# Layer norms 5 and 6 of a two-layer decoder in halves by batch, and the last products between turned rows

## The chip, the cores and the metric

The kernel runs on one core of a Trainium2 chip. The metric is the device time of one execution in microseconds. A core has a matrix engine (TensorE, PE), a vector engine (DVE), a scalar engine (ScalarE, ACT), GpSimd (POOL) and a queue of transfers (SyncE, SP); each works through its own list of instructions in order and waits on semaphores.

## The reference

`x` is 8 batches of 128 rows by 512 columns, in fp32. Six sublayers are added to it, each over a layer norm:

```
def _layernorm(x, axis=-1, eps=1e-05):
    m = jnp.mean(x, axis=axis, keepdims=True)
    v = jnp.var(x, axis=axis, keepdims=True)
    return (x - m) / jnp.sqrt(v + eps)
...
    x = x + _L0_attn_ref(_layernorm(x, axis=-1), ...)
    x = x + _L0_xattn_ref(_layernorm(x, axis=-1), ctx_4096, mask_BxSxS2_bk0, fside_Bx32xSxS2_0, ...)
    x = x + _L0_ffn_ref(_layernorm(x, axis=-1), ...)
    x = x + _L1_attn_ref(_layernorm(x, axis=-1), ...)
    x = x + _L1_xattn_ref(_layernorm(x, axis=-1), ctx_4096, ctx_4096, ...)
    x = x + _L1_ffn_ref(_layernorm(x, axis=-1), ...)
```

The fifth sublayer is a cross attention with 32 heads of 16 columns (8 key groups of 4 heads), scores, softmax and an output product. The sixth unpacks a 512x512 weight from 3 bits, multiplies the normed x with it and adds a bias. The fourth ends with a root mean square norm over the attention output, applied here as one scale per row (`y_scale`).

## The kernel before

**Numbers as pairs.** Every operand of a large product is split in a rounded high part and the low rest. `mm3` makes a product of three matmuls: high by high, high by low, low by high. A product of 128 rows by 512 columns over K = 512 is thus 12 matmuls. ScalarE writes a high part (`hi`, `turned`, `weight_hi`), the vector engine subtracts it for the low part (`lo`); for weights in SBUF, GpSimd does that (`split_lo`, one instruction over 128x1024).

**Layer norms** are numbered 0 to 5 in the code; the title's fifth and sixth are 4 and 5. Before, norms 4 and 5 run whole. `stats` (bn_stats) is taken per batch after its addition; when all eight are there, `deviation` makes eight aggregations and one `var_eps`, ScalarE the square root, the vector engine the reciprocal (`normed`). Then for each batch b: the vector engine writes the normed row block to one of two buffers (`probs` 0 and 1), TensorE turns it (four transposes in a bank `pj`, `turn`), ScalarE writes `xt_hi`, the vector engine `xt_lo`, which frees the bank. Norms 1 to 3 already go in halves of four batches (`half_deviation`, `half_rstd`); their order is written out by hand.

**Order of the end of the fourth sublayer (L883 to L932, L1281 to L1292, L1868 to L1887).** TensorE finishes the last head pair between the key and value products of the fifth: `tail`, `sums` (the sum of squares per row), `keys(hf, m)`, four transposes of the values. The vector engine adds `y_scale` times y to x (`add_scaled`, one per batch). GpSimd sums the squares of two heads (`both_heads`), splits weights of slots 3, 0, 1, 2 and 4, then makes the first two blocks of masked keys (`block_keys`), and behind the last addition clears and fills the padded values. TensorE then turns rows 0 to 3, makes `queries(0, 0)`, turns rows 4 and 5, `queries(0, 1)`, rows 6 and 7, `queries(0, 2)`, `scores(0)`, `queries(0, 3)`.

**The loop of the fifth sublayer** has 16 iterations n (batch n // 2, half of the key groups n % 2), each with four groups g: scores of iteration n + 1 (TensorE), `row_max` (vector), `exps` (ScalarE), `row_sums` and reciprocal (vector), `normalise` (GpSimd), `transposes` (TensorE), `turned_out` (ScalarE), `values` (TensorE). In even n from 2 on `output(n // 2 - 1)` is a product of 12 matmuls, added to x by the vector engine with its bn_stats (`add`); in odd n `heads` copies the attention output as a pair. `block_keys(n + 2)` is the last GpSimd instruction but the padding in an iteration. `dequantise(part)` makes a quarter of the 3 bit weight in three vector instructions (0 and 1 before the loop, 2 and 3 in iterations 0 and 1). Weights of `l1x_o` (slot 3) get their low part on the vector engine in front of the first row sums.

**The end (L1043 to L1056).** After values(15) TensorE turns the weight's quarters 0 and 1 (`turned_weights`), makes output(7), turns quarters 2 and 3, then all eight rows of norm 5, and then eight products, each added to x by the vector engine and sent out by the SP queue. Two banks `ou` alternate. The bias is added for all batches ahead of the first product's addition:

```
            normed(5)
            for b in range(B):
                dve.tensor_tensor(X[:, b, :], X[:, b, :], BIAS[:], ALU.add).then_inc(bias_added, 1)
            for b in range(B):
                n, bank = nth(OU["l1f"], 0, 0, b)
                dve.wait_ge(bias_added, b + 1)
                add_output(n, bank, X[:, b, :])
```

Of the kernel before, what the change touches and what calls it, by code (L numbers as in the profile page):

```python
# [92 lines left out]
LNV = [0, 1, 3, 5, 7, 8]  # L93
# [15 lines left out]
def build(nc, a):  # L109
    ctx = ExitStack()  # L110
    with ctx:
# [280 lines left out]
        def _(pool):  # L392
# [96 lines left out]
            split_lo(4, SLOT["l1x"][4])  # L489
# [27 lines left out]

            block_keys(0)
            block_keys(1)
            pool.wait_ge(la_y, B)  # L520
# [4 lines left out]
            pad_values(0)  # L525
            for g in range(KG):
                normalise(0, g)
# [10 lines left out]
        def _(pe):  # L538
# [392 lines left out]
            keys(1, 0)  # L931
            pe.wait_ge(la_v, 3)  # L932
            keys(1, 1)

# [75 lines left out]

            def turned_weights(c):
# [9 lines left out]
            turn(4, range(0, 4))  # L1021
# [4 lines left out]
            turn(4, range(4, 6))  # L1026
            queries(0, 1)
            turn(4, range(6, B))
            queries(0, 2)
            scores(0)  # L1030
            queries(0, 3)
            for n in range(NG):
# [6 lines left out]
                if n % 2 == 0 and n:  # L1039
                    output(n // 2 - 1)  # L1040
                values(n)
                for c in {5: (0,), 6: (1,), 7: (2, 3)}.get(n, ()):
                    queries(1, c)  # L1043
            turned_weights(0)
            turned_weights(1)
            output(B - 1)
            turned_weights(2)
            turned_weights(3)
            layer_norm(5)
            for b in range(B):  # L1050
                n, bank = nth(OU["l1f"], 0, 0, b)
                pe.wait_ge(pj_done, PJ["ln5"] + b + 1)
                ou_free(n)
                for c in range(KC):
                    last = mm3(ou[bank][:], rows(XT, b)(c), wrows(L1F_SLOTS)(c), c == 0, c == KC - 1)
                last.then_inc(ou_full, 1)  # L1056
# [3 lines left out]
        def _(act):  # L1060
# [220 lines left out]
            scale_std(1)  # L1281
# [3 lines left out]
            deviation(4)  # L1285
            for f in range(2):
                n, bank = nth(PJ["l1xv"], 0, 0, 2 + f)
                act.wait_ge(pj_full, n + 1)
                act.activation(AF[:, V1 + f * HALF:V1 + (f + 1) * HALF], pj[bank][:], ACT.Copy).then_inc(pj_done, 1)
            act.wait_ge(kr_full, 2)  # L1290
# [35 lines left out]
            turned(4, range(6))  # L1326
            queries(0, 0)
            turned(4, range(6, B))
            queries(0, 1)
            queries(0, 2)  # L1330
# [23 lines left out]
            for g in range(KG):  # L1354
                turned_out(NG - 1, g)
            heads(B - 1)

# [7 lines left out]
            deviation(5)  # L1365
            weights_hi(2)
            weights_hi(3)
            turned(5, range(B))
# [3 lines left out]
        def _(dve):  # L1372
# [495 lines left out]
            for n in range(HB):  # L1868
# [7 lines left out]
                l1a_step(None, (HG - 1, 1), "O", n)  # L1876
            for b in range(HB):
                stats(b)
            mean_square(1)
            scaled(1)  # L1880
            for b in range(HB, B):
                add_scaled(b)
# [34 lines left out]
            for g in range(KG):  # L1917
                row_max(0, g)
# [125 lines left out]
```

## Time and profile before

| | us |
|---|---|
| median of three runs | 2473.59 (2472.96 to 2476.45) |
| the profiled execution | 2473.39 |
| its span | 2471.6 |
| PE busy | 2366.2 |
| DVE busy | 1256.2 |
| ACT busy | 902.2 |
| POOL busy | 668.5 |

The profile comes from one execution. Busy times are shares of the span from the first to the last instruction; matmuls are pipelined, so a busy TensorE isn't one at its peak. In a row of the timeline, "idle" in brackets is how long the engine did nothing before it, and behind the arrow stands what ended that. The granted clock is TensorE's, as a share of 2.4 GHz; 0.50 is 1.2 GHz.

### The profile page before, as it was taken

How to read it: one execution, taken by the hardware profiler on the slowest of the kernel's cores; microseconds unless marked ns; L12 is line 12 of the kernel's file. 1: busy time of each engine (PE TensorE's matmuls, PEld its weight loads, DVE VectorE, ACT ScalarE, POOL GpSimd, SP SyncE). 2: the span in 40 equal slices, each digit the busy share in tenths (PEclk: the TensorE clock that was granted, in tenths of full speed). 3: DMA queues.
4: the chain of work that ended last, by engine and by line, in shares of the span. 5: the costliest groups of instructions: out<-in, count | busy, mean ns of one | idle time of the engine just before them, and what ended most of it. 6: DMA issues, size and time to landing. Idle time of an engine off the chain costs nothing.

```text
span 2471.6 us, 38446 instructions
## 1 busy us (share of the span) xinstructions
PE 2366.2 (96%) x13227; PEld 2019.0 (82%) x13227; DVE 1256.2 (51%) x2917; ACT 902.2 (37%) x2230; POOL 668.5 (27%) x383
## 2 busy tenths in 40 slices
PE   5999899999999999998999999999999999997888
PEld 3788688888888889887888888888888888886555
DVE  6444644445444444456644444444444444457765
ACT  2111344444444444443233333333333333334763
POOL 4434522322222322231311111111111111112550
PEclk9999999999999999999999999999999999998888
DMA  3110212111111211110111111111111111100000
GB/s 117 68 43 26 103 52 74 61 51 58 61 51 60 76 51 51 68 60 27 49 41 45 45 45 45 45 45 45 45 45 45 45 45 45 45 18 0 1 1 35
DMA packets 36831, 118.96 MB, mean 48 GB/s; under 512 B 4904, under 2 KB 7336, under 8 KB 36784
## 3 DMA queue, kind: packets, MB, share of 16 engines
q1 hardware_dynamic: 36784, 118.35, 14.1%
q8 instruction: 28, 0.46, 0.1%
q14 instruction: 19, 0.16, 0.0%
HBM read 116.24 MB, written 2.10 MB: 48 GB/s over the span
## 4 chain that ended last, share of the span: by engine, by line
PE 87%; DVE 6%; issue 3%; POOL 2%; ACT 1%; SPq 0%; DMA 0%; POOLq 0%; ACTq 0%; DVEq 0%
PE pj L542 19%; PE pj L543 18%; PE pj L544 18%; PE ou L542 6%; PE ou L544 6%; PE ou L543 6%; PE pv L720 2%; PE sc L857 2%; PE pv L866 2%; PE sc L704 2%; PE tp L711 1%; POOL w_lo L410 1%; DVE neg_max L1891 1%; POOL w_hi L408 1%; DVE probs L1424 1%
## 5 line engine op out<-in xcount | busy, mean ns | idle before, releaser
L402 POOL TENSOR_TENSOR w_lo<-raw,w_hi 128x1024 fp32r<-128x1024 f32 x145 | 346.6, 2391 | 1438.0 <-ACT w_hi L1094 1398.6
L542 PE MATMUL pj<-xt_hi,w_hi 128*128 128x512 f32 x1232 | 498.8, 405 | 6.2 <-DVE xt_lo L1459 2.4
L543 PE MATMUL pj<-xt_lo,w_hi 128*128 128x512 f32 x1232 | 482.1, 391 | 0.0
L544 PE MATMUL pj<-xt_hi,w_lo 128*128 128x512 f32 x1232 | 481.7, 391 | 0.0
L542 PE MATMUL ou<-w_hi,act_hi 128*128 128x512 f32 x684 | 274.7, 402 | 0.8 <-DVE x L1383 0.6
L542 PEld LDWEIGHTS pj<-xt_hi,w_hi 128*128 128x128 f32 x1232 | 233.0, 189 | 50.0 <-DVE xt_lo L1459 2.6
L544 PEld LDWEIGHTS pj<-xt_hi,w_lo 128*128 128x128 f32 x1232 | 232.0, 188 | 49.5
L544 PE MATMUL ou<-w_hi,act_lo 128*128 128x512 f32 x684 | 267.6, 391 | 0.0
L543 PE MATMUL ou<-w_lo,act_hi 128*128 128x512 f32 x684 | 266.8, 390 | 0.0
L543 PEld LDWEIGHTS pj<-xt_lo,w_hi 128*128 128x128 f32 x1232 | 233.0, 189 | 40.8
L1383 DVE TENSOR_TENSOR x<-x,ou 128x512 f32<-128x512 f32 x192 | 130.8, 684 | 254.6 <-PE ou L544 254.2
L1245 ACT ACTIVATE side<-pj 128x512 f32<-128x512 f32 (+1 forms) x256 | 125.6, 491 | 341.1 <-PE pj L544 341.0
L1821 DVE TENSOR_TENSOR queries_keys<-side,pj 128x512 f32<-128x512 f32 x128 | 88.1, 688 | 184.6 <-ACT side L1245 184.6
L1160 ACT ACTIVATE queries_keys<-pj 128x512 f32<-128x512 f32 x128 | 76.5, 598 | 245.2 <-PE pj L544 245.2
L542 PE MATMUL pj<-w_hi,xt_hi 128*128 128x256 f32 (+1 forms) x544 | 160.7, 295 | 2.5 <-DVE x_sum L1461 1.6
L1094 ACT ACTIVATE w_hi<-raw 128x1024 fp32r<-128x1024 f32 x146 | 153.5, 1051 | 20.5 <-PE ou L544 18.7
L542 PEld LDWEIGHTS ou<-w_hi,act_hi 128*128 128x128 f32 x684 | 128.9, 188 | 36.6 <-issue 10.7
L543 PE MATMUL pj<-w_lo,xt_hi 128*128 128x256 f32 (+1 forms) x544 | 157.4, 289 | 0.0
L544 PE MATMUL pj<-w_hi,xt_lo 128*128 128x256 f32 (+1 forms) x544 | 157.4, 289 | 0.0
L544 PEld LDWEIGHTS ou<-w_hi,act_lo 128*128 128x128 f32 x684 | 128.7, 188 | 27.8
L543 PEld LDWEIGHTS ou<-w_lo,act_hi 128*128 128x128 f32 x684 | 129.0, 189 | 24.4
L542 PE MATMUL pj<-w_hi,ctx_hi 128*128 128x256 f32 x512 | 147.8, 289 | 0.7 <-POOL w_lo L410 0.7
(241 smaller groups left out, 4553.1 us busy)
## 6 DMA issues: line engine op xcount, KB each, us to landing
raw<-in_l1a_w SPq DMA_DIRECT2D x80, 512.0 KB, 4.2
raw<-in_l0x_w SPq DMA_DIRECT2D x64, 512.0 KB, 4.3
side<-in_side SPq DMA_DIRECT2D x32, 512.0 KB, 3.9
raw<-in_ffn_w SPq DMA_DIRECT2D x15, 512.0 KB, 3.3
raw<-in_l0f_w SPq DMA_DIRECT2D x6, 512.0 KB, 3.7
raw<-in_l1x_w SPq DMA_DIRECT2D x6, 512.0 KB, 3.8
raw<-in_taylor_w SPq DMA_DIRECT2D x5, 512.0 KB, 7.3
x<-in_x SPq DMA_DIRECT2D x2, 1024.0 KB, 6.6
```

Of the source, the lines that this page charges most:

```text
L402: pool.tensor_tensor(WL[:, s, :], RAW[:, s, :], f32(WH[:, s, :]), ALU.subtract).then_inc(w_ready[s], 1)
L542: pe.matmul(out, wh, xh, start=first, stop=False)
L543: pe.matmul(out, wh, xl, start=False, stop=False)
L544: return pe.matmul(out, wl, xh, start=False, stop=last)
L704: last = pe.matmul(score(j)[:, h * S:(h + 1) * S], heads_of(0, h, j), heads_of(1, h, j), start=True, stop=True)
L720: last = pe.matmul(pv[:, h * S:(h + 1) * S], VT[:, n, h * S:(h + 1) * S], TA[:, n % 2, h * S:(h + 1) * S], start=True, stop=True)
L857: last = pe.matmul(score(j)[:, h * S:(h + 1) * S], heads_of(1, h, j), heads_of(0, h, j), start=True, stop=True)
L1094: act.activation(WH[:, s, :], RAW[:, s, :], ACT.Copy).then_inc(w_hi[s], 1)
L1160: act.activation(QK[:, n, :], bank[:], ACT.Copy, scale=S ** -0.5 if n < 2 else 1.0).then_inc(pj_done, 1)
L1245: act.activation(F[:, x % 2, 0:w], pj[bank][:, 0:w], ACT.Sigmoid).then_inc(la_sg, 1)
L1383: dve.tensor_tensor(dst, dst, ou[bank][:], ALU.add).then_inc(x_done, 1)
L1821: dve.tensor_tensor(dst, F[:, x % 2, 0:w], pj[bank][:, 0:w], ALU.mult).then_inc(pj_done, 1)
```

## The change

Norms 4 and 5 get two halves of four batches each. `LNV`, the count of deviations before each norm, becomes `[0, 1, 3, 5, 7, 9]`. On TensorE:

```diff
             keys(1, 0)
+            turn(4, range(2))
             pe.wait_ge(la_v, 3)
             keys(1, 1)
+            turn(4, range(2, HB))
...
+            def product(b):
+                bank = (b + 1) % 2
+                pe.wait_ge(pj_done, PJ["ln5"] + b + 1)
+                if b:
+                    pe.wait_ge(x_done, OU["l1f"] + b - 1)
+                else:
+                    pe.wait_ge(tn_out, NG * KG)
+                for c in range(KC):
+                    last = mm3(ou[bank][:], rows(XT, b)(c), wrows(L1F_SLOTS)(c), c == 0, c == KC - 1)
+                last.then_inc(ou_full, 1)
...
-            turn(4, range(0, 4))
             pe.wait_ge(pj_done, PJ["ln4"] + HB)
...
             queries(0, 0)
-            turn(4, range(4, 6))
             queries(0, 1)
-            turn(4, range(6, B))
+            turn(4, range(HB, HB + 2))
             queries(0, 2)
+            turn(4, range(HB + 2, B))
             scores(0)
...
                     output(n // 2 - 1)
+                if n + 1 == NG:
+                    turned_weights(0)
+                    turned_weights(1)
                 values(n)
...
-            turned_weights(0)
-            turned_weights(1)
-            output(B - 1)
             turned_weights(2)
             turned_weights(3)
-            layer_norm(5)
+            turn(5, range(2))
+            output(B - 1)
             for b in range(B):
...
+                if b + 2 < B:
+                    turn(5, (b + 2,))
+                product(b)
```

On GpSimd the split of slot 4 moves behind the first padding, and both key blocks behind all eight additions:

```diff
             split_lo(2, SLOT["l1x"][2])
-            split_lo(4, SLOT["l1x"][4])
...
+            pool.wait_ge(la_y, B)
             block_keys(0)
             block_keys(1)
-            pool.wait_ge(la_y, B)
...
             pad_values(0)
+            split_lo(4, SLOT["l1x"][4])
             for g in range(KG):
                 normalise(0, g)
```

On ScalarE:

```diff
-            scale_std(1)
             act.wait_ge(kr_full, 1)
             for m in range(2):
                 keys_out(0, m)
-            deviation(4)
+            half_deviation(4, 0)
+            scale_std(1)
...
+            turned(4, range(HB))
             act.wait_ge(kr_full, 2)
...
-            turned(4, range(6))
             queries(0, 0)
-            turned(4, range(6, B))
+            half_deviation(4, 1)
             queries(0, 1)
+            turned(4, range(HB, B))
             queries(0, 2)
...
-            for g in range(KG):
-                turned_out(NG - 1, g)
-            heads(B - 1)
-
+            turned_out(NG - 1, 0)
+            turned_out(NG - 1, 1)
+            half_deviation(5, 0)
+            turned_out(NG - 1, 2)
+            turned_out(NG - 1, 3)
...
             weights_hi(1)
-            deviation(5)
+            heads(B - 1)
             weights_hi(2)
             weights_hi(3)
-            turned(5, range(B))
+            turned(5, range(3))
+            half_deviation(5, 1)
+            turned(5, range(3, B))
```

On the vector engine, at norm 4 (`turn_row` writes a normed row, `turn_lo` the low part of a turned one):

```diff
-                l1a_step(None, (HG - 1, 1), "O", n)
+                if n < HB - 1:
+                    l1a_step(None, (HG - 1, 1), "O", n)
...
             for b in range(HB):
                 stats(b)
+            half_deviation(4, 0)
+            l1a_step(None, (HG - 1, 1), "O", HB - 1)
             mean_square(1)
+            half_rstd(4, 0)
+            turn_row(4, 0)
+            turn_row(4, 1)
             scaled(1)
-            for b in range(HB, B):
-                add_scaled(b)
+            add_scaled(4)
+            turn_lo(4, 0)
+            turn_row(4, 2)
+            turn_lo(4, 1)
+            turn_row(4, 3)
+            add_scaled(5)
+            turn_lo(4, 2)
+            turn_lo(4, 3)
+            add_scaled(6)
+            add_scaled(7)
             for b in range(HB, B):
                 stats(b)
-            deviation(4)
-
-            normed(4)
+            half_deviation(4, 1)
+            half_rstd(4, 1)
+            turn_row(4, 4)
+            turn_row(4, 5)
+            turn_lo(4, 4)
...
```

Around the loop and at the end:

```diff
             dequantise(0)
-            dequantise(1)
             for g in range(KG):
                 row_max(0, g)
+            for g in range(KG):
+                row_sums(0, g)
             dve.wait_ge(w_hi[3], SLOT["l1x_o"] + 1)
             dve.tensor_tensor(WL[:, 3, :], RAW[:, 3, :], f32(WH[:, 3, :]), ALU.subtract).then_inc(w_ready[3], 1)
-            for g in range(KG):
-                row_sums(0, g)
...
-                if n in (0, 1):
-                    dequantise(2 + n)
+                if n in (0, 1, 3):
+                    dequantise((0, 1, 3).index(n) + 1)
...
+                if n + 2 == NG:
+                    half_deviation(5, 0)
                 row_sums(n + 1, 2)
...
-            heads(B - 1)
...
+            half_rstd(5, 0)
+            turn_row(5, 0)
+            turn_row(5, 1)
             weights_lo(0)
             weights_lo(1)
+            heads(B - 1)
             weights_lo(2)
             weights_lo(3)
+            turn_lo(5, 0)
+            turn_row(5, 2)
+            turn_lo(5, 1)
+            turn_row(5, 3)
+            add(B - 1)
+            half_deviation(5, 1)
+            turn_lo(5, 2)
+            half_rstd(5, 1)
+            turn_row(5, 4)
+            add_bias(0)
+            add_bias(1)
+            turn_lo(5, 3)
+            turn_row(5, 5)
+            add_product(0)
+            turn_lo(5, 4)
+            turn_row(5, 6)
+            add_bias(2)
+            add_product(1)
...
```

and so on, one low part, one row, one bias and one product a step, to `add_product(7)`.

## Rows read from the trace of the kernel before

**Rows 1.** The page, part 1: busy us (share of the span) and instructions.
```profile
PE 2366.2 (96%) x13227; PEld 2019.0 (82%) x13227; DVE 1256.2 (51%) x2917; ACT 902.2 (37%) x2230; POOL 668.5 (27%) x383
```
**Rows 2.** Table by stage: us, busy PE, PEld, DVE, ACT, POOL, clock, DMA.
```profile
2240.00:2256.00 16.00, 8.67 (x37) 6.42 (x35) 14.18 (x30) 5.41 (x12) 6.44 (x8) 0.79 0.00 1
```
**Rows 3.** Timeline, all engines, norm 4 to scores(1): start, us, engine, line, operation.
```profile
2238.01 2.46 DVE L1866 BATCH_NORM_STATS2 bn_stats<-x 128x6 f32<-128x512 f32 x4
2238.53 4.75 POOL L402 TENSOR_TENSOR w_lo<-raw,w_hi 128x1024 fp32r<-128x1024 f32 x2 [1.60 <-ACT w_hi L1094]
...
2241.01 5.52 DVE L1861 SCALAR_TENSOR_TENSOR x<-y,y_scale,x 128x512 f32<-128x512 f32 x4
...
2250.92 1.97 PE L565 MATMUL pj<-identity,probs 128*128 128x128 f32 x8 [6.36 <-DVE probs L1424]
...
2257.09 0.79 PE L542 MATMUL ou<-xt_hi,w_hi 128*128 128x512 f32 x1 [1.41 <-DVE xt_lo L1377]
...
2262.38 1.36 PE L565 MATMUL pj<-identity,probs 128*128 128x128 f32 x8
...
2266.31 1.04 PE L565 MATMUL pj<-identity,probs 128*128 128x128 f32 x8
...
2271.71 1.28 ACT L1309 ACT_TABLE_LOAD   x1
...
2280.00 0.80 PE L967 MATMUL sc<-keys_blocked,act_whole 32*128 32x256 f32 x2
```
**Rows 4.** Timeline of GpSimd in the loop: the key blocks.
```profile
2280.85 0.61 POOL L497 TENSOR_TENSOR keys_blocked<-keys_whole,block_mask 128x256 f32<-128x256 f32 x1
...
2302.07 0.61 POOL L497 TENSOR_TENSOR keys_blocked<-keys_whole,block_mask 128x256 f32<-128x256 f32 x1
...
2310.26 0.61 POOL L497 TENSOR_TENSOR keys_blocked<-keys_whole,block_mask 128x256 f32<-128x256 f32 x1
...
2326.40 0.61 POOL L497 TENSOR_TENSOR keys_blocked<-keys_whole,block_mask 128x256 f32<-128x256 f32 x1
```
**Rows 5.** Timeline of the last stage, all engines.
```profile
2421.58 0.60 ACT L1318 ACTIVATE turned_whole<-tp 128x512 f32<-128x512 f32 x1 [1.38 <-PE tp L981]
...
2423.23 1.77 PE L995 MATMUL pv<-turned_whole,values_padded 128*32 128x512 f32 x8 [0.69 <-ACT turned_whole L1318]
...
2424.93 1.97 PE L1018 MATMUL pj<-identity,w 128*128 128x128 f32 x8
...
2429.74 0.69 DVE L1383 TENSOR_TENSOR x<-x,ou 128x512 f32<-128x512 f32 x1 [1.49 <-PE ou L544]
...
2434.91 1.97 PE L565 MATMUL pj<-identity,probs 128*128 128x128 f32 x8 [4.33 <-DVE probs L1424]
...
2468.48 0.69 DVE L1383 TENSOR_TENSOR x<-x,ou 128x512 f32<-128x512 f32 x1 [2.03 <-PE ou L544]
```
**Rows 6.** Vector engine by line, 2434 to 2472: busy us, mean ns, idle.
```profile
L1377 DVE TENSOR_TENSOR xt_lo<-pj,xt_hi 128x512 fp32r<-128x512 f32 x8 | 5.5, 689 | 1.4 <-ACT xt_hi L1064 1.2
...
L1951 DVE TENSOR_TENSOR x<-x,bias 128x512 f32<-128x512 f32 x8 | 4.9, 684 | 0.0
L1424 DVE TENSOR_SCALAR probs<-x,bn_mean_var,rstd 128x512 f32<-128x512 f32 x8 | 4.3, 542 | 1.2 <-PE pj L565 1.2
```
**Rows 7.** Timeline of vector engine and GpSimd at norm 1.
```profile
256.55 0.38 DVE L1437 BATCH_NORM_AGGREGATE bn_mean_var<-bn_stats 128x2 f32<-128x6 f32 x4
256.96 1.03 DVE L1441 TENSOR_SCALAR var_eps<-bn_mean_var 128x4 f32<-128x4 f32 x1
...
256.08 1.88 POOL L416 TENSOR_TENSOR ctx_hi<-side,one 128x1024 fp32r<-128x1024 f32 x1
```
**Rows 8.** Table by single us, columns as in rows 2.
```profile
2422.00:2423.00 1.00, 0.54 (x4) 0.30 (x4) 0.00 (x0) 0.60 (x2) 0.00 (x0) 1.00 0.00 0
2423.00:2424.00 1.00, 0.77 (x8) 0.16 (x8) 0.00 (x0) 0.17 (x1) 0.00 (x0) 0.73 0.00 0
...
2447.00:2448.00 1.00, 1.00 (x5) 0.78 (x5) 1.00 (x3) 0.00 (x0) 0.00 (x0) 0.83 0.00 0
```

More of the change, by code:

```diff
@@ L1043, in _ @@
                     queries(1, c)
-            turned_weights(0)
-            turned_weights(1)
-            output(B - 1)
             turned_weights(2)
             turned_weights(3)
-            layer_norm(5)
+            turn(5, range(2))
+            output(B - 1)
             for b in range(B):
[L1051 to L1056, printed above, removed]
+                if b + 2 < B:
+                    turn(5, (b + 2,))
+                product(b)
         @block.scalar
@@ L1940, in weights_lo, with add_bias, add_product @@
                 lo(fill, HI["l1f"] + c, wpair(WL, L1F_SLOTS, c, 512), pj[fill[1]][:], wpair(WH, L1F_SLOTS, c, 512))
+            def add_bias(b):
+                dve.wait_ge(ln_x, 5 * B + b + 1)
+                dve.tensor_tensor(X[:, b, :], X[:, b, :], BIAS[:], ALU.add).then_inc(bias_added, 1)
+            def add_product(b):
+                dve.wait_ge(bias_added, b + 1)
+                add_output(OU["l1f"] + b, (b + 1) % 2, X[:, b, :])
+            half_rstd(5, 0)
+            turn_row(5, 0)
+            turn_row(5, 1)
             weights_lo(0)
             weights_lo(1)
-            add(B - 1)
-            dve.wait_ge(x_done, OU["l1f"])
-            deviation(5)
+            heads(B - 1)
             weights_lo(2)
             weights_lo(3)
-            normed(5)
-            for b in range(B):
-                dve.tensor_tensor(X[:, b, :], X[:, b, :], BIAS[:], ALU.add).then_inc(bias_added, 1)
-            for b in range(B):
-                n, bank = nth(OU["l1f"], 0, 0, b)
-                dve.wait_ge(bias_added, b + 1)
-                add_output(n, bank, X[:, b, :])
+            turn_lo(5, 0)
[16 more added lines that the diff above has]
+            add_product(1)
+            turn_lo(5, 5)
+            turn_row(5, 7)
+            add_bias(3)
+            add_product(2)
+            turn_lo(5, 6)
+            add_bias(4)
+            add_product(3)
+            turn_lo(5, 7)
+            add_bias(5)
+            add_product(4)
+            add_bias(6)
+            add_product(5)
+            add_bias(7)
+            add_product(6)
+            add_product(7)
 def arr(a):
```

16 lines of the change are left out of this document (15 added, 1 removed).

## The prediction

> **What bounds the kernel now.** I read the page first: TensorE is busy 96% of the span [rows 1]. The change touches nothing before 2215 us, though, so this average says little. The table by stage shows where TensorE isn't the bound [rows 2]: around layer norm 4 (the code's number) it is busy 8.67 of 16 us, the vector engine 14.18. Then the timeline of the first stage [rows 3], to see who releases whom: TensorE is idle for 6.36 us, from 2244.56 until the first turned row at 2250.92, and once more before the queries (2257.09), of which the first product then takes 5.3 us, until 2262.38. The reader sees that the vector engine holds it up: its four additions end at 2246.5, and four statistics, aggregation, deviation and rows follow. Then the loop by GpSimd's key blocks, one an iteration [rows 4], and the last stage [rows 5]: TensorE waits 4.33 us for row 0, turns eight rows in 10 us at the half clock and at the pace of a ring (turn, high part, low part, next row), and only then makes eight products at a pitch of 2.72 us (the 2.03 and 0.69 of the last row).
>
> All times are on the clock of the profiled execution: 2473.39 us for a span of 2471.6, 0.2 us under the median of 2473.59. The 1.8 us around the span and the 3.1 from the last addition to its end I take as unchanged.
>
> **Stage 1, layer norm 4 in halves.** Removed is the one norm behind all additions; added are two half norms with a deviation each. In order:
> - The first four statistics start at 2238.01 behind a y addition, which moves behind them: now 2237.4 to 2239.9, and with four aggregations 2240.35 [rows 3, 7]. Next is var_eps, while GpSimd splits slot 2 (2238.53 to 2240.9, half of its row). Such an instruction waits until GpSimd's ends [rows 7]: 2241.0.
> - y addition (0.7) and mean square: 2241.95; reciprocal and rows 0, 1 (0.54 each, [rows 6]): 2243.15. TensorE turns them between keys(1,0) and keys(1,1) (2.8 us each, so from 2241.7 on), by 2243.65; keys(1,1) ends at 2246.45 and rows 2 and 3 at 2247.35, 0.45 a row and less at full clock (the 1.04 for two).
> - High part 0.6, low part 0.69, the second low part 0.7 behind: 2248.95. queries(0,0) starts there instead of at 2257.09 and takes 2.8 us at full clock; with queries(0,1) 2254.5.
> - GpSimd's split of slot 4 and its two key blocks are out of the additions' way: two SBUF inputs cost them 1.38 each there, 0.70 free. The last ends at 2250.3, the statistics at 2252.75, the aggregation at 2253.1.
> - But GpSimd starts at 2250.3 as well: two key blocks (0.61 each when alone, [rows 4]), two clears and two paddings (1.2 in all), and split_lo(4), 2.4 us, from about 2252.75 to 2255.15. The second var_eps comes at 2253.1 and is held until 2255.2. These 2 us lie on the path.
> - Root, reciprocal, rows 4 and 5: 2256.7; turned 2257.2; queries(0,2) to 2259.95; rows 6 and 7 turned by 2260.85; last low part 2262.3, for which scores(0) waits, now as then.
> - ScalarE copies queries(0,2) and makes a weight (1.05), so its table load starts at 2263.3 against 2271.71, and the first exponentials at 2264.85. The row sums follow at once, no longer behind w_lo (1.2 us). GpSimd's second normalisation ends at 2270.05, and scores(1) starts at 2270.8 against 2280.00: **9.2 us gained** at the loop's door. w_lo(3) has its reader two iterations on. dequantise(1) stood ahead of the first maxima, but under the table load: taking it away there gains nothing.
>
> Bounds: half clock for queries(0,0) (2.5) and the turned rows (1.2): 5.5. No hold, and scores(1) 0.7 sooner: 11.8.
>
> **Stage 2, the loop.** dequantise stands in iterations 0, 1 and 3, not 0 and 1. Two iterations with it take 21.22 us (key blocks at 2280.85 and 2302.07), two without 16.14 (2310.26 and 2326.40): 2.54 each, of which the half clock may have a part. Two of its three instructions last 0.69 as in [rows 6]; with 1.4 the lower end. I take 2.5 lost; the upper end is 3.1. half_deviation(5,0) puts 0.55 us before the last two row sums of iteration 14; stage 3 carries it. GpSimd is idle at that point.
>
> **Stage 3, the end.** On the old axis:
> - The 0.55 moves the last two normalisations to 2421.4 and 2422.4. ScalarE's root, with a table load (1.28), fills 2420.2 to 2421.7, inside the 1.38 us that it idles before a copy [rows 5]; that copy is ready at 2422.1. Hidden; without that idle time 1.5.
> - turned_weights(0) and (1) go ahead of values(15). At the half clock, as now [rows 5, 8], they take 1.97, to 2425.1; values(15), ready at 2423.8, ends at 2426.9.
> - heads(7) ends at 2428.15 on the vector engine, and the low parts of weights 2 and 3 are queued behind it: 2428.85, 2429.5. Rows 0 and 1 need their banks, and are turned by 2429.35 and 2430.0. Behind them on TensorE stands output(7): to 2432.8, now 2429.7. Three us given up.
> - Row 2 is turned at 2433.25, and product(0) starts there, not at 2444.5. A product costs 2.73 and a turned row 0.45: 3.2 us a step up to product(5) at 2449.25, then 2452.0, 2454.7, end 2457.45, while the last addition now starts at 2468.48, 0.1 behind its product. Ten us of turning become 6 x 0.45.
> - The vector engine's work of a step is 0.69+0.54+0.61+0.69 = 2.5 of 3.2 us [rows 5, 6], so hidden. But there is a ring: product(b) ends, row b+3 is turned (0.45), high (0.6), low (0.69), next row, bias and addition (1.85), and after 3.65 to 3.8 us product(b+2) may write the bank, where TensorE arrives after 3.65. I charge 0.2 in all: 10.9 - 0.2 = **10.7 us gained**, the 0.55 included.
>
> Bounds: half clock over output(7) (2.4) and 0.15 a step in the ring: 7.5. Full clock at the turned weights (1.5): 12.2.
>
> **Sum.** 9.2 - 2.5 + 10.7 = 17.4; 2473.39 - 17.4 = 2456.0 us. The worst ends give 5.5 - 3.1 + 7.5 = 9.9 (2463.5), the best 11.8 - 1.4 + 12.2 = 22.6 (2450.8).
>
> **Rivals.**
> A. split_lo(4) doesn't hold var_eps, because it starts behind it: 1.9 more, **2454.1**. For it: the two starts are 0.35 us apart. Against: what GpSimd does ahead of the split is as long as four statistics. 10%.
>
> B. The clock falls in the gaps. It fell at 2423.3, after a stretch in which TensorE worked in pieces (0.54 of the last us), and at 2249, idle since 2244.56; it returned at 2447.2, the engine at work since 2443 [rows 3, 8]. The new stage 1 has gaps of 1.6 and 1.8 us, the new end 1.2. At the half clock queries(0,0) costs 2.5 more and output(7) 2.4: **2460.9**. 25%. The Trainium skill, TensorE: Matmul & The Clock Gate, in its section on the second failure mode of the gate, says that short idles between groups of matmuls can make the clock go up and down. By that rule both losses come; the row at 2423 is in line with it. The gap that cost the clock in stage 1 was 6.36 us long, though, and hence no more than 25%.
>
> C. The ring of stage 3 is slower: a pitch of 3.8 instead of 3.2 us over six products, 3.6 more: **2459.6**. For it: less than 0.1 us of slack a step. Against: the bias is free to run ahead. 10%.
>
> D. Slower than before: turning in between keeps the half clock over the products. One then costs 5.1 instead of 2.73 (queries(0,0) took 5.3), a row 1.0 instead of 0.45: 8 x 2.4 + 6 x 0.55 = 22.5 more, **2478.5**. It decides from the sixth such product on (17.4 / 2.95). Against: TensorE has work without a gap there, and in the same place it came back 2.8 us into the products [rows 8]. 2%.
>
> E. The first half of layer norm 4 comes no earlier than all eight rows now, since eight instructions stand ahead of it: stage 1 gives nothing, so 8.2 in all, **2465.2**. Against: its rows are due at 2243.15, 7 us before today's. 3%.
>
> My sum has the other 50%.
>
> **Numbers.** Forecast 2456.0; from 2451.0, the best ends, to 2463.0, which holds A, B and C and leaves out D, E and some of the worst ends. A measurement of this kernel can tell about 0.2%, 5 us: faster by more (under 2468.6) 0.95, within it 0.03, slower 0.02.
>
> **What would show it.** queries(0,0) near 2249 at 0.23 us a matmul; the second var_eps lasting 2 us beside split_lo(4); the table load near 2263; iteration 3 some 2.5 us longer. At the end eight products at 3.2 us, the first at 2426.6 (2433.25 less 9.2 plus 2.5). It is wrong if queries(0,0) lasts 5 us, if the pitch is over 3.4, or if scores(1) comes less than 6 us earlier.

## The result and the profile after

| | before | after |
|---|---|---|
| median of the executions (each over 4) | 2473.28 us (2470.65 to 2476.45) | 2458.77 us (2455.03 to 2460.19) |
| the profiled execution | 2473.39 us | 2459.67 us |
| its span | 2471.6 us | 2457.8 us |

The ratio is 0.9932, with a 95% interval of 0.9920 to 0.9945: 16.8 us faster by the ratio, 14.5 by the medians. Four more executions of the changed kernel, in a later run, gave 2456.30 us (2453.91 to 2456.72) and 0.9925 (0.9908 to 0.9941). The forecast was 2456.0 us.

The page of after has the same load on every engine but TensorE, as it should, for no product was added or taken away (part 1, answers to [rows 1]); what went is idle time and time at the half clock.

```profile
PE 2358.6 (96%) x13227; PEld 2012.9 (82%) x13227; DVE 1255.9 (51%) x2921; ACT 902.7 (37%) x2232; POOL 668.3 (27%) x383
```

The two profiled executions are 4.26 us apart before the first changed instruction: the split of slot 1 (GpSimd's w_lo behind its first sum of squares) starts at 2218.49 before and at 2222.75 after. So I read every stage from that split on, not from the span's start. The timeline of stage 1 after, all engines, answers to [rows 3, 7]:

```profile
2244.56 0.63 DVE L1455 TENSOR_SCALAR var_eps<-bn_mean_var 128x4 f32<-128x4 f32 x1
...
2246.72 1.11 PE L565 MATMUL pj<-identity,probs 128*128 128x128 f32 x8 [0.64 <-ACT act_whole L1299]
...
2253.05 0.50 PE L542 MATMUL ou<-xt_hi,w_hi 128*128 128x512 f32 x1 [1.57 <-DVE xt_lo L1391]
...
2256.66 2.38 POOL L402 TENSOR_TENSOR w_lo<-raw,w_hi 128x1024 fp32r<-128x1024 f32 x1
...
2257.14 1.92 DVE L1455 TENSOR_SCALAR var_eps<-bn_mean_var 128x4 f32<-128x4 f32 x1
...
2260.15 1.11 PE L565 MATMUL pj<-identity,probs 128*128 128x128 f32 x8 [1.37 <-DVE probs L1896]
...
2266.56 0.48 PE L969 MATMUL sc<-keys_blocked,act_whole 32*128 32x256 f32 x2 [1.67 <-DVE xt_lo L1391]
...
2267.03 1.28 ACT L1320 ACT_TABLE_LOAD   x1
```

The reader sees the 6.36 us wait of TensorE gone: rows 0 and 1 are turned 0.64 us after TensorE came free, and the waits left are 1.57, 1.37 and 1.67. The second var_eps, an instruction over four columns, lasts 1.92 us, to the end of GpSimd's split. The table of the 16 us around the norm, the same stretch as in [rows 2] moved by 4.26, has TensorE busy 12.41 us instead of 8.67, at full clock:

```profile
2244.26:2260.26 16.00, 12.41 (x61) 9.60 (x61) 14.52 (x33) 5.83 (x13) 5.47 (x8) 1.00 0.00 1
```

GpSimd's key blocks in the loop after, against [rows 4]: from the first to the third 20.01 us (21.22 before), from there to the fifth 17.21 (16.14 before, from the fourth block to the sixth).

```profile
2277.35 0.61 POOL L496 TENSOR_TENSOR keys_blocked<-keys_whole,block_mask 128x256 f32<-128x256 f32 x1
...
2297.36 0.61 POOL L496 TENSOR_TENSOR keys_blocked<-keys_whole,block_mask 128x256 f32<-128x256 f32 x1
...
2306.57 0.61 POOL L496 TENSOR_TENSOR keys_blocked<-keys_whole,block_mask 128x256 f32<-128x256 f32 x1
...
2314.57 0.61 POOL L496 TENSOR_TENSOR keys_blocked<-keys_whole,block_mask 128x256 f32<-128x256 f32 x1
```

The end after, all engines, answers to [rows 5]. L1031 are the turned weights, L997 is values(15), L565 the turned rows:

```profile
2417.59 1.28 ACT L1087 ACT_TABLE_LOAD   x1
...
2418.88 0.21 ACT L1087 ACTIVATE std<-var_eps 128x4 f32<-128x4 f32 x1
...
2420.23 1.04 PE L1031 MATMUL pj<-identity,w 128*128 128x128 f32 x8
...
2421.20 1.06 PE L997 MATMUL pv<-turned_whole,values_padded 128*32 128x512 f32 x8
...
2424.46 1.23 PE L565 MATMUL pj<-identity,probs 128*128 128x128 f32 x8 [0.90 <-DVE w_lo L1391]
...
2428.30 0.60 PE L565 MATMUL pj<-identity,probs 128*128 128x128 f32 x4
...
2431.51 0.60 PE L565 MATMUL pj<-identity,probs 128*128 128x128 f32 x4
...
2437.91 0.60 PE L565 MATMUL pj<-identity,probs 128*128 128x128 f32 x4
...
2441.30 0.60 PE L565 MATMUL pj<-identity,probs 128*128 128x128 f32 x4
...
2453.59 0.69 DVE L1397 TENSOR_TENSOR x<-x,ou 128x512 f32<-128x512 f32 x1 [2.03 <-PE ou L544]
```

The turned weights take 1.04 us, not 1.97. The wait of 4.33 us is 0.90, and the eight rows no longer stand together: one is turned every 3.21 us with a product between, once 3.39. The vector engine by line, 2420 to 2455, against [rows 6]: the same instructions at the same price, with more idle time ahead of the low parts (5.4 us) and none ahead of the bias or the rows.

```profile
L1391 DVE TENSOR_TENSOR xt_lo<-pj,xt_hi 128x512 fp32r<-128x512 f32 x8 | 5.5, 689 | 5.4 <-ACT xt_hi L1074 5.4
L1990 DVE TENSOR_TENSOR x<-x,bias 128x512 f32<-128x512 f32 x8 | 5.4, 684 | 0.0
L1896 DVE TENSOR_SCALAR probs<-x,bn_mean_var,rstd 128x512 f32<-128x512 f32 x7 | 3.8, 538 | 0.0
```

The table by single us has the clock at full in the very stretch where it fell before [rows 8] (the columns as there):

```profile
2418.00:2419.00 1.00, 0.26 (x2) 0.26 (x3) 0.32 (x2) 0.99 (x2) 1.00 (x2) 1.00 0.00 0
2421.00:2422.00 1.00, 1.00 (x11) 0.19 (x9) 0.45 (x1) 1.00 (x3) 0.00 (x0) 1.00 0.00 0
2425.00:2426.00 1.00, 1.00 (x8) 0.89 (x8) 0.25 (x1) 0.87 (x2) 0.00 (x0) 1.00 0.00 0
```

### The profile page after: what moved, and what is told of

It is laid out like the page before. It is cut to its first block, busy times and chain, and to the rows that moved or that the text cites. A ratio compares the mean times of both kernels' runs of the same rounds, so it can differ in the third digit from the quotient of the medians.

```text
span 2457.8 us, 38454 instructions
## 1 busy us (share of the span) xinstructions
PE 2358.6 (96%) x13227; PEld 2012.9 (82%) x13227; DVE 1255.9 (51%) x2921; ACT 902.7 (37%) x2232; POOL 668.3 (27%) x383
## 4 chain that ended last, share of the span: by engine, by line
PE 88%; DVE 5%; issue 3%; POOL 2%; ACT 1%; SPq 0%; DMA 0%; POOLq 0%; ACTq 0%; DVEq 0%
PE pj L542 19%; PE pj L543 19%; PE pj L544 19%; PE ou L542 6%; PE ou L544 6%; PE ou L543 6%; PE pv L720 2%; PE sc L857 2%; PE pv L866 2%; PE sc L704 2%; PE tp L711 1%; POOL w_lo L410 1%; POOL w_hi L408 1%; PE sc L969 1%; DVE neg_max L1938 1%
## 5 line engine op out<-in xcount | busy, mean ns | idle before, releaser
L544 PEld LDWEIGHTS pj<-xt_hi,w_lo 128*128 128x128 f32 x1232 | 232.6, 189 | 49.7
L1104 ACT ACTIVATE w_hi<-raw 128x1024 fp32r<-128x1024 f32 x146 | 153.5, 1052 | 20.5 <-PE ou L544 18.7
L542 PEld LDWEIGHTS ou<-w_hi,act_hi 128*128 128x128 f32 x684 | 128.7, 188 | 36.6 <-issue 10.7
```

What stands on the lines that cost most here:

```text
L542: pe.matmul(out, wh, xh, start=first, stop=False)
L544: return pe.matmul(out, wl, xh, start=False, stop=last)
L1104: act.activation(WH[:, s, :], RAW[:, s, :], ACT.Copy).then_inc(w_hi[s], 1)
```

## The experiments

I cut every profiled execution at four instructions: the start of the split of slot 1, the first matmul of scores(1), GpSimd's first normalisation for values(15) (2416.78 before, 2414.15 after), and the last addition. "Half" is the time in the stage with TensorE at the half clock, worked out from the tables by single us as twice the sum of 1 minus the granted clock.

```
kernel                        split at  start  loop (half)   end (half)  rest
before                        2218.49   61.51  136.78 44.5  51.70 17.0    3.1
before, again                 2221.69   61.42  135.05 34.1  50.92 13.7    3.1
changed                       2222.75   52.72  138.68 49.8  39.44  0.0    4.2
changed, again                2219.66   52.75  138.41 49.5  39.44  0.0    4.2
norm 4 alone                  2220.65   52.73  138.57 49.7  51.67 17.1    3.1
norm 5 and end alone          2217.83   61.43  134.99 34.1  40.78  3.4    3.1
split of slot 4 late          2218.43   50.65  134.85 34.1  41.01  3.4    3.1
GpSimd's old order            2219.73   52.56  138.41 49.5  39.45  0.0    3.8
quarters in 5, 7, 9           2219.58   52.79  138.52 49.5  39.44  0.0    3.1
quarter 0 in the gap          2221.88   54.07  135.61 37.6  40.76  3.4    3.1
weights behind values(15)     2221.47   52.74  138.63 49.7  44.06  6.8    3.1
rows ahead of the products    2219.48   52.74  138.42 49.5  44.96  3.4    3.1
late split, 5, 7, 9           2219.63   50.68  137.08 44.4  39.43  0.0    3.1
late split, quarter in gap    2220.50   56.51  138.11 49.1  39.43  0.0    3.1
```

**Both kernels once more.** No edit.

> The changed kernel, unchanged. Theory: the gain of 13.7 us in the first profiled pair is 18.1 by stages (8.8 up to scores(1), -1.9 in the loop, 11.2 at the end) less 4.26 us by which the profiled execution was late already at 2218 us, and that lateness is chance: a second profiled execution has GpSimd's first split w_lo (L402, behind both_heads of the last pair) anywhere from 2217 to 2224 us, while the three stages repeat within 0.3 us each. Rival: the change itself costs 4 us ahead of its own place (a longer program); then the split starts at 2222.5 to 2223.5 again.

> The kernel before, unchanged, for its own spread. In the profiled execution of before the loop took 136.78 us with TensorE's clock at half for 44.5 us; the kernel with only the end changed, whose code is the same up to iteration 14, took 134.99 with 34.1. Theory: which stretches of the loop run at half is settled from execution to execution by small shifts, so this one has any of 34, 37, 41 or 44 us at half, and 134.9 to 136.9 for the loop in step. Rival: it is fixed by the kernel; then 136.7 to 136.9 and 44.5 again. Start 61.5 and end 51.7 in both.

Measured: 2456.30 us for the changed kernel and 2474.19 for the one before, which is 1.0001 (0.9991 to 1.0011) of itself. The changed kernel's three stages repeat to 0.3 us, and the split is at 2219.66 this time. For the kernel before it is at 2221.69, later than at first. The 4 us ahead of the change are chance, and the rival that the change costs them falls. The end of the kernel before took 50.92 us this time, not the 51.7 expected, with 3.3 us less at the half clock. On its loop the theory holds: with not a line changed it took 135.05 us with 34.1 at half, against 136.78 with 44.5. The table by single us of this second execution shows where they part, 7 us into the loop:

```profile
2289.00:2290.00 1.00, 0.53 (x8) 0.16 (x8) 1.00 (x2) 1.00 (x5) 0.00 (x0) 0.96 0.00 0
2290.00:2291.00 1.00, 1.00 (x8) 0.00 (x0) 0.93 (x5) 1.00 (x6) 0.63 (x1) 0.50 0.00 0
2293.00:2294.00 1.00, 1.00 (x14) 0.71 (x15) 0.00 (x0) 0.66 (x2) 1.00 (x2) 0.83 0.00 0
2295.00:2296.00 1.00, 0.62 (x6) 0.38 (x4) 1.00 (x3) 0.78 (x3) 0.00 (x0) 1.00 0.06 16
```

The clock falls at 2290 and is back at 2293.3. In the first execution, 3.2 us earlier throughout, the same fall came at 2287 and lasted until 2293.7.

**Norm 4 alone, norm 5 alone.** The first has norm 5 whole and the old end, the second the old start:

```diff
@@ norm 4 alone: TensorE, and the other engines alike
-                if n + 1 == NG:
-                    turned_weights(0)
-                    turned_weights(1)
...
+            layer_norm(5)
@@ norm 5 alone: the vector engine, and the other engines alike
-            half_deviation(4, 0)
...
+            deviation(4)
+            normed(4)
```

> Norm 4 in halves, GpSimd's order and dequantise as in the changed kernel; norm 5 whole and the end as in the kernel before. Theory (stages add up): 8.8 - 1.9 = 6.9 us faster than before, about 2466.5 to 2467; from the last normalisation but one to the end 51.7 us as before. Rival 1: the end isn't independent (the clock at the end hangs on norm 4's side or the halves of norm 5 overlap what was won): the end takes 2 us more or less than 51.7. Rival 2: the lateness at 2218 us comes with the new end's instructions; then it is gone here.

> Start of the fifth sublayer, norm 4, dequantise and GpSimd's order as in the kernel before; norm 5 in halves, turned weights ahead of values(15) and the products between turned rows as in the changed kernel. Theory: 11.2 us faster than before, about 2462; the end 40.5 us. Rival: the full clock at the turned weights (the changed kernel has 0.99 there, the kernel before 0.5) hangs on the loop's phase; then the turned weights take 1.97 us instead of 1.04 and the end is 41.5 to 43 us: 2463 to 2464.5.

Measured: 2469.05 us, 0.9978 (0.9967 to 0.9988), 5.6 less than before (6.9 expected); and 2461.60 us, 0.9951 (0.9934 to 0.9967), 13.1 less. Together 18.7, where the whole change gave 18.4 against the same executions of before. The parts add up. Norm 4 alone has start 52.73 and the old end of 51.67: its rivals fall. Norm 5 alone wins by more than the 11.2 expected. Between its profile and the first of before, the end gives 10.9 us and the loop 1.8, in which it ran at half for only 34.1 us. The turned weights ran at half, as the rival has it, but the end of 40.78 stays close to the theory's 40.5 and under the rival's 41.5 to 43 (timeline of TensorE in that kernel):

```profile
2420.93 1.83 PE L1029 MATMUL pj<-identity,w 128*128 128x128 f32 x8
```

**The split of slot 4.**

```diff
@@ late split
             pad_values(0)
+            pool.wait_ge(ln_x, 5 * B)
             split_lo(4, SLOT["l1x"][4])
@@ GpSimd's old order
             split_lo(2, SLOT["l1x"][2])
+            split_lo(4, SLOT["l1x"][4])
...
-            pool.wait_ge(la_y, B)
             block_keys(0)
             block_keys(1)
+            pool.wait_ge(la_y, B)
```

> The changed kernel, but GpSimd waits for the deviation of norm 4's second half before it splits slot 4. Theory: var_eps took 1.92 us only because GpSimd's split (2.38 us) held it; now it takes 0.1 to 0.2, rows 4 to 7 and scores(0) come 1.7 us sooner, and as slot 4 isn't needed before output(0) nothing waits for the split unless it holds the first normalisation: scores(1) 1.0 to 1.7 us sooner on the axis of the first split. Rival 1: the 1.9 us are hidden behind queries(0,1) (TensorE idled only 1.37 us there), so 0.5 to 1.4. Rival 2: the split, now from 2257.3 to 2259.7, holds the next two-input work of the vector engine instead, no gain (within 0.3).

> The changed kernel with GpSimd's order as before: split of slot 4 right behind slot 2, key blocks ahead of the wait for the additions. Theory of the prediction: the second var_eps is no longer held (1.9 us less), but the rows 0 and 1 of the first half are now beside the split (they start 1.2 to 1.6 us later) and two of the additions beside the key blocks (0.7 more each), so scores(0) comes -0.7 to +1.0 us against the 43.8 after the first split. Rival: the hold is all there is to it, 1.7 us earlier, as in the kernel whose split comes late. Rival 2: the additions' 0.7 and the rows come all on the path: 1.5 to 3 us later.

The late split is released by norm 4's last row, not by its deviation, as the expectation has it. The timeline of that kernel:

```profile
2252.84 0.17 DVE L1456 TENSOR_SCALAR var_eps<-bn_mean_var 128x4 f32<-128x4 f32 x1
...
2257.89 2.35 POOL L402 TENSOR_TENSOR w_lo<-raw,w_hi 128x1024 fp32r<-128x1024 f32 x1 [5.49 <-DVE probs L1897]
```

The same var_eps takes 0.17 us, scores(0) starts 1.66 us sooner after the first split (42.19 against 43.85), and scores(1) 2.10 sooner, more than the 1.0 to 1.7 expected; the last 0.4 of it go with 1.7 us of half clock ahead of scores(1), which this kernel lacks. That the hold lies on the path is shown. The median is 2450.32 us, 0.9907 (0.9888 to 0.9925), 6.0 under the changed kernel on the same chip. That is more than the 2.1. Between the spans of the two profiled executions 6.3 us are 1.2 ahead of the cut, 2.1 in the start, 3.6 in the loop and 1.0 in the rest, less 1.6 in the end: the loop's half clock lasted 34.1 us instead of 49.5, while not a line of it was changed.

GpSimd's old order gave 2456.00 us (0.9928, 0.9913 to 0.9943), within 0.2 us of the changed kernel at every cut. Its timeline shows the hold at another place:

```profile
2239.74 4.72 POOL L402 TENSOR_TENSOR w_lo<-raw,w_hi 128x1024 fp32r<-128x1024 f32 x2 [1.58 <-ACT w_hi L1104]
...
2242.95 2.55 DVE L1896 TENSOR_SCALAR probs<-x,bn_mean_var,rstd 128x512 f32<-128x512 f32 x2
...
2255.51 0.17 DVE L1455 TENSOR_SCALAR var_eps<-bn_mean_var 128x4 f32<-128x4 f32 x1
```

Rows 0 and 1 end at 2245.5 with the split of slot 4's own end at 2244.46 in between: 2.55 us instead of 1.00. The second var_eps is free. What one half wins the other pays, so reordering GpSimd's list as the change did brought nothing by itself (0.2 us the other way).

The Trainium skill, in SBUF — State Buffer, section "SBUF: two separate sides", has the vector engine and GpSimd share one pair of ports, which is locked for a whole instruction, and not divided. The rows agree: 1.92 and 0.63 us for an instruction that takes 0.17 alone, each up to the end of GpSimd's.

**The quarters of the 3 bit weight.** The prediction charged the loop 2.5 us for one more quarter in it.

```diff
@@ quarters in 5, 7, 9
-                if n in (0, 1, 3):
-                    dequantise((0, 1, 3).index(n) + 1)
+                if n in (5, 7, 9):
+                    dequantise((5, 7, 9).index(n) + 1)
@@ quarter 0 in the gap
             turn_row(4, 7)
+            dequantise(0)
             turn_lo(4, 6)
...
-            dequantise(0)
+            dequantise(1)
...
-                if n in (0, 1, 3):
-                    dequantise((0, 1, 3).index(n) + 1)
+                if n in (0, 1):
+                    dequantise(2 + n)
```

> The changed kernel, its quarters 1, 2 and 3 of the 3 bit weight in iterations 5, 7 and 9 instead of 0, 1 and 3. Theory of the prediction: one quarter costs its iteration 2.5 us, so the key blocks of iterations 0 to 2 come 16.2 to 17 us apart instead of 19.9 and those of iterations 5, 7 and 9 each 2.5 us later than now. Second theory, from the runs so far (with the clock at half for 34.1 us of the loop the kernel with two quarters inside took 134.99 us and the one with three 134.85; with 44.5 and 49.5 us at half 136.78 and 138.41): a quarter costs under 0.4 us anywhere, the first iterations are long for another reason and stay at 19.3 to 20.5 us together, and the loop differs from 138.4 only with the time at the half clock.

> The changed kernel, with quarter 0 of the 3 bit weight in a gap of the vector engine ahead of norm 4's row 6, quarter 1 ahead of the loop, 2 and 3 in iterations 0 and 1. By the prediction's term (2.5 us for a quarter in the loop) the loop falls to 136 us and the total by 1.5 to 2.2 us. By the second theory (a quarter costs nothing there) the start changes by -0.3 to +0.5 us and the loop by no more than its time at the half clock brings (0.2 to 0.35 us for each us).

Quarters in iterations 5, 7 and 9: 2454.23 us, 0.9916 (0.9900 to 0.9933). The loop takes 138.52 us, as with the quarters in 0, 1 and 3, and the first iterations stay long without them (GpSimd's key blocks, 19.79 us from the first to the third):

```profile
2274.24 0.61 POOL L496 TENSOR_TENSOR keys_blocked<-keys_whole,block_mask 128x256 f32<-128x256 f32 x1
...
2294.03 0.61 POOL L496 TENSOR_TENSOR keys_blocked<-keys_whole,block_mask 128x256 f32<-128x256 f32 x1
```

The term of the prediction falls. Quarter 0 in the gap: 2456.92 us, 0.9927 (0.9910 to 0.9944), no gain. Its loop is 2.8 us shorter, which alone would look like the 2.5; but the table by stage of the loop tells of another cause. One row for each execution, from scores(1) to the normalisation. The kernel before, with two quarters inside:

```profile
2280.00:2416.78 136.78, 112.55 (x716) 71.88 (x716) 99.40 (x200) 96.78 (x302) 69.85 (x85) 0.84 0.00 1
```

The same kernel again:

```profile
2283.11:2418.16 135.05, 108.39 (x714) 69.73 (x714) 99.45 (x200) 97.09 (x302) 69.81 (x86) 0.87 0.00 1
```

Norm 5 and the end alone, two quarters as well:

```profile
2279.26:2414.25 134.99, 108.40 (x714) 69.71 (x714) 99.45 (x200) 97.08 (x302) 69.80 (x85) 0.87 0.00 1
```

And the late split, with three:

```profile
2269.08:2403.93 134.85, 108.64 (x714) 69.90 (x714) 102.50 (x206) 97.16 (x302) 71.22 (x87) 0.87 0.00 1
```

With the clock at 0.87 the loop takes 134.99 and 135.05 us with two quarters and 134.85 with three, though the vector engine is 3 us busier. At 44.5 us of half clock it is 136.78 with two and 137.08 with three; at 49.1 to 49.8 it is 138.11 with two and 138.4 to 138.7 with three. A quarter costs -0.2 to +0.6 us; each us at the half clock costs (138.41 - 134.85) / 15.4 = 0.23.

In the gap kernel, the start is 1.3 us longer, which neither theory had. The first exponentials are only 0.4 us later; what is late is the copy of queries(0,3) (2271.64, 49.76 after the split, against 47.98), whose product fell under a half clock from 2266.3 on.

**Both ideas together.**

> The changed kernel with the late split of slot 4 and the quarters of the weight in iterations 5, 7 and 9. Theory: a quarter costs nothing wherever it stands, so this equals the kernel with the late split alone: start 50.65, loop 134.9 (34 us at half), end 39.4 to 41, 2450 to 2452 us. Rival: the 134.85 us of that kernel was an accident of one execution: loop 138.4 and 49.5 us at half as in all five kernels with the same start but one, 2453 to 2455.

> Late split of slot 4 with quarter 0 in the vector engine's gap, quarter 1 ahead of the loop, 2 and 3 in iterations 0 and 1. Theory: start 50.65 + 1.3 (quarter 1 delays the first maxima, as it did in the kernel with the gap) = 52.0, loop 134.8 to 135.7 at 34 to 38 us of half clock, end 39.4 to 40.8: 2451 to 2453. Rival (the prediction's term of 2.5 us a quarter): the loop 2.5 us shorter than with the late split alone, 132.4: 2448 to 2450.

Late split with the quarters in 5, 7 and 9: 2453.96 us over 5 executions (2448.81 to 2457.46), 0.9917 (0.9904 to 0.9931). The start repeats (50.68). The loop does neither: 137.08 us with 44.4 at half, between theory and rival, and the five times spread over 8.6 us. The 34.1 of the late split alone weren't fixed by its code. Over both kernels with the late split, nine executions have a median of 2452.4 us; the sixteen of the three with a start of 52.6 to 52.8 us and the new end in full (the changed one, GpSimd's old order, quarters in 5, 7 and 9) 2456.2. The granted clock over the whole of each execution is on record, and orders the five times: 0.991 for 2448.81 us, 0.988 for 2452.42 and 2453.96, 0.987 for 2454.45, 0.985 for 2457.46. At equal clock, from 0.987 to 0.990, the kernels with the late split lie 1.1 to 5.2 us under those three by their medians, 2.3 at 0.990. So I take some 2 us of the 3.8 as shown (stage 1), the rest as the clock's luck; whether the earlier start helps the clock isn't shown.

Late split with quarter 0 in the gap: 2459.69 us, 0.9941 (0.9927 to 0.9954), worse than either, and outside both expectations. The timeline of that kernel shows why:

```profile
2260.00 2.47 POOL L402 TENSOR_TENSOR w_lo<-raw,w_hi 128x1024 fp32r<-128x1024 f32 x1 [5.57 <-DVE probs L1897]
...
2260.29 2.73 DVE L1517 TENSOR_TENSOR w<-w,q_norm 128x512 f32<-128x512 f32 x1
```

The split, freed by the last row, starts just before the product w times q_norm that I had put behind that row, and holds it for 2 us ahead of the low part that scores(0) needs: 44.59 instead of 42.19. In the longer gap the clock fell (8.9 us at half in the start, none in the late split alone), and scores(1) is 5.9 us late.

**The end.**

```diff
@@ weights behind values(15)
-                if n + 1 == NG:
-                    turned_weights(0)
-                    turned_weights(1)
                 values(n)
...
+            turned_weights(0)
+            turned_weights(1)
             turned_weights(2)
@@ rows ahead of the products
+            turn(5, range(2, B))
             for b in range(B):
-                if b + 2 < B:
-                    turn(5, (b + 2,))
                 product(b)
```

> The changed kernel, with the weight's quarters 0 and 1 turned behind values(15), as before. Theory: the two now fill a wait of TensorE for the copy that values(15) reads (0.7 to 1.0 us), so the end grows by 0.7 to 1.1 us, at the full clock. Rival: in that wait the clock falls, as in the kernel before, and the turned weights and output(7) run at half: 1.0 for the weights and up to 2.4 for the product on top, the end 3 to 4.5 us longer.

> The changed kernel, but all rows of norm 5 are turned ahead of the first product; halves and early weights as they are. Theory: six rows (2 to 7) go by the ring of turn, high part, low part over two banks, 1.2 to 1.3 us each, so the first product starts 6.5 us later while each step loses its 0.45 of turning: the end 3.5 to 5 us longer than 39.4. Rival: with TensorE in pieces for 7 us the clock falls, as in the kernel before, and comes back only some us into the products: 8 to 11 us longer. Third: the halves alone brought the gain, and the alternation is worth under 1 us.

Weights behind values(15): 2461.80 us, 0.9945 (0.9929 to 0.9962), the end 4.6 us longer with 6.8 at half. It is the rival, just above its 3 to 4.5, though what ran at half was values(15) and turned blocks, and not output(7). The fastest of the four executions, 2457.30 us, had a granted clock of 0.990, the others 0.985 to 0.987: the loss isn't in every execution. TensorE's timeline in that kernel:

```profile
2419.76 1.94 PE L997 MATMUL pv<-turned_whole,values_padded 128*32 128x512 f32 x8 [0.69 <-ACT turned_whole L1328]
...
2421.63 1.70 PE L1031 MATMUL pj<-identity,w 128*128 128x128 f32 x8
...
2424.16 1.25 PE L1031 MATMUL pj<-identity,w 128*128 128x128 f32 x8 [0.83 <-DVE w_lo L1390]
...
2426.31 1.93 PE L565 MATMUL pj<-identity,probs 128*128 128x128 f32 x8 [0.90 <-DVE w_lo L1390]
```

The wait of 0.69 us that the turned weights had filled is back, values(15) and the first weights run at half, the rows 0 and 1 once more. But the second execution of before had the same wait of 0.69 and its values(15) at full clock (1.06 us), and norm 5 and the end alone had the wait filled and its weights at half. Over all fourteen profiles, the four without the filling have the fall at values(15) in three, whose loops ran at half for 44.5 to 49.7 us, and not in the one with 34.1. The ten with it have the fall at the weights in the three with 34.1 to 37.6 us, and not in the seven with 44.4 to 49.8. So whether the clock falls there goes with the loop's pattern as well as with the filling, and the filling doesn't forbid it.

Rows ahead of the products: 2460.35 us, 0.9945 (0.9928 to 0.9962), the end 5.5 us longer with 3.4 at half. TensorE's timeline there:

```profile
2424.75 1.04 PE L565 MATMUL pj<-identity,probs 128*128 128x128 f32 x8
...
2428.30 0.66 PE L565 MATMUL pj<-identity,probs 128*128 128x128 f32 x4 [2.51 <-DVE probs L1895]
...
2429.35 0.66 PE L565 MATMUL pj<-identity,probs 128*128 128x128 f32 x4 [0.40 <-DVE probs L1895]
...
2430.82 2.17 PE L565 MATMUL pj<-identity,probs 128*128 128x128 f32 x8 [0.81 <-DVE probs L1895]
```

TensorE waits 3.72 us in all for row 4 (behind the second half's deviation) and those after it, and the clock falls at 2431 for the last two. The theory's 3.5 to 5 is just missed; the third view, that the alternation is worth under 1 us, falls. Of the end's 12.3 us, the alternation holds 5.5 and the early weights 4.6, each measured with the other present, in one profile each, and with the half clock that came with it (3.4 and 6.8 us).

## Why the prediction came out right, point by point

The cuts give for the two profiled executions 8.8 (start) - 1.9 (loop) + 12.3 (end) - 1.1 (rest) - 4.3 (ahead of the change) = 13.8 us. Forecast were 9.2 - 2.5 + 10.7, with the rest as before and nothing ahead. The second profile of each kernel gives 8.7 - 3.4 + 11.5 - 1.1 + 2.0 = 17.7: the loop and the end of the kernel before differ between its own two profiles by 1.7 and 0.8 us.

- **Stage 1, 9.2 forecast, 8.8 measured.** Less the shift of 4.26 each: queries(0,0) at 2248.79 (forecast 2248.95) at full clock, second var_eps held for 1.92 us (2.0), table load 2262.77 (2263.3), scores(1) 2271.21 (2270.8). The 0.4 missing: the exponentials waited 0.52 us behind the table load for the maxima, since quarter 0 stands ahead of them. I had the table load as the last to end.
- **The loop, 2.5 lost forecast, 1.9 and 3.4 measured, for another reason.** This step failed. I took the difference between two iterations with a quarter (21.22 us) and two without (16.14) for the quarters' price. But the first iterations ran at half for 12.9 us against 3.4, and are as long with no quarter in them. A quarter fits in the vector engine's idle time, but for 0.6 us at most. Of the 1.9 us, 5.3 us more of half clock make up some 1.2 at 0.23 each; the 3.4 of the second pair go with 15.4 us more. Iteration 3 isn't 2.5 us longer either: the key blocks around its quarter are 8.00 us apart (2306.57 to 2314.57), and 8.64 in the kernel with the quarters in 5, 7 and 9, which has none there. Since the kernel before itself has either 34.1 or 44.5 us at half, the term should have been 0 to 0.6 for the quarter, with a range of some 2 us in both directions for the clock. Why the loop of the changed kernel runs at half for 49.5 us stays open.
- **The end, 10.7 forecast, 12.3 and 11.5 measured.** The mechanism was right: the product begins between the rows, a step is 3.21 us (3.2), the ring cost 0.2 once (0.2 in all). Mis-sized was the term of the turned weights, charged at the half clock with 1.97 us; they took 1.04, and values(15) and the rows ran at full clock as well. The first product started at 2428.65, or 2424.4 less the shift, where the forecast had 2426.6. My bound for full clock at the weights was 12.2. The root's table load was hidden, as said.
- **Rest, taken as unchanged.** From the last addition to the end it was 4.2 us in two executions of the changed kernel, 3.8 in one of another and 3.1 in all others, among them kernels with the same end. The difference is in the last transfer of x, which landed 3.1 us after its issue in the changed kernel and 2.0 in the kernel before. An earlier one of the eight took 4.2 in the kernel before, so a late landing isn't new; no run tells why this one is late.
- **Rivals.** A (no hold) falls by the row of 1.92. B (half clock in the new gaps) didn't come in the changed kernel, but three kernels show falls of the clock close by: weights behind values(15) in the end, both with quarter 0 in the gap in stage 1. C (a pitch of 3.8) falls: 3.21, once 3.39. D falls, as no product ran at half. E falls: the rows 0 and 1 were turned (2250.92 - 2218.49) - (2246.72 - 2222.75) = 8.5 us sooner after the split.
- **Readings.** By [rows 8] the clock fell at 2423.5 (0.73 in that us) and returned at 2447.3 (0.83), not at 2423.3 and 2447.2. Nothing in the sum hangs on it.

That the median came within 3 us of the forecast is in part luck. The stages of the first pair give 19.2 us where 17.4 were forecast, and the rest and the shift ahead of the change took some 5.3 back; the loop's term came near its measure for a wrong reason.

The Trainium skill, in TensorE: Matmul & The Clock Gate, section "A second HAM failure mode: psum-queue depth-cycling", says that short idles between groups of matmuls can swing the clock. I gave this 25% for the changed kernel. The loop, with its short waits, swings in all fourteen executions, from 34 to 50 us at half, so the trace agrees there; behind the gaps of 1.57, 1.37 and 1.67 us in stage 1 after, the clock stayed full until 2274.0, 1.5 us ahead of scores(1).

## What to carry to other kernels

Before a stage is compared between two kernels, compare it between two executions of one: cut both at the same instructions, and set the time at the half clock beside each stage's length. A short iteration next to a long one isn't the price of the instruction that only the long one has, as long as the clock differs between them. And a large GpSimd instruction is to be started where the vector engine reads PSUM or takes statistics, not next to the small instruction on which a norm hangs. Four statistics took 2.46 us beside a split [rows 3] and as long without one; two low parts read from PSUM 1.29 us beside the late split and without; but a small or a two-input instruction in the wrong place went from 0.17 us to 1.92, and from 0.69 to 2.73.

## What the runs showed that I had not expected

- Two executions of the same kernel had the loop at half for 44.5 and 34.1 us (136.78 and 135.05 us long). Six kernels with a start of 52.6 to 52.8 us, the changed one twice, all had 49.5 to 49.8. So some starts repeat their pattern well and others don't.
- A table load of ScalarE cost its own 1.28 us and no more: the one at 2417.59 is followed by the root at 2418.88. Nor was there a wait ahead of it where ScalarE came straight from another ACTIVATE: in the changed kernel's stage 1 a weight's high part ends at 2267.02 and the load starts at 2267.03.
- The time up to 2218 us, in code that no kernel here changes, differs by up to 4.9 us between executions (2217.83 to 2222.75), more than the effect of most edits above. In the first pair most of it is the clock again. Of its 4.26 us, 1.2 were there by 42 us, at the input's transfers. The rest came in two stretches that ran at half in the profile after and at full clock in the one before: 301.1 to 304.5, behind which the shift is 2.7 us, and 1103.3 to 1106.7, behind which it is 4.3. Table by stage over the first of them, before and then after:

```profile
301.10:304.50 3.40, 3.40 (x20) 2.93 (x19) 0.69 (x1) 1.76 (x3) 0.47 (x1) 1.00 0.02 5
```

```profile
301.10:304.50 3.40, 3.40 (x10) 2.61 (x9) 1.02 (x4) 0.18 (x1) 0.00 (x0) 0.51 0.11 41
```
